# Folding layer norm and the q/k/v projection into one-hot tables, with the slots of a step filled anew and the stack loads moved to mid-step

## What is computed

```python
nesting, segments = _syntax_info(ids)              # two small integers per token: 16 and 8 values
h = concat(pos_table[s], nest_table[nesting], seg_table[segments]) @ W
qkv = layernorm(h) @ qkv_w.T + qkv_b               # 8 heads of 16 channels
attn = softmax(q @ k.T / 4)                        # 512 x 512 per head
h = h + (attn @ v) @ out_w.T + out_b
h = h + mixture_of_4_experts(layernorm(h))         # relu, low rank, gates
```

## Time and profile before

| | before |
|---|---|
| median of 3 runs | 1200.86 us |
| the profiled execution's own time | 1200.39 us |
| its span (first to last instruction) | 1198.6 us |
| PE busy | 1112.8 us, 93% of the span |
| DVE busy | 910.2 us, 76% |
| ACT busy | 823.0 us, 69% |
| POOL busy | 592.8 us, 49% |
| granted TensorE clock, mean | 0.973 |

### The profile page before, as it was taken

One profiled execution on the slowest core, in us unless ns is written; L12 is line 12 of the kernel. 1 busy time (PEld: TensorE's weight loads), 2 busy tenths in 40 slices (PEclk: granted clock), 3 DMA queues, 4 the chain that ended last, 5 costly groups with the idle time before them and its releaser, 6 DMA issues.

```text
span 1198.6 us, 20409 instructions
## 1 busy us (share of the span) xinstructions
PE 1112.8 (93%) x6392; PEld 455.6 (38%) x6392; DVE 910.2 (76%) x2370; ACT 823.0 (69%) x1602; POOL 592.8 (49%) x588
## 2 busy tenths in 40 slices
PE   2579999999999999999999999999999999999975
PEld 1223334444344434434344444443443444433322
DVE  6288888877888788777888887778888877788322
ACT  0217777777777777777777777777777777777841
POOL 2644555456544555565445655654455555622231
PEclk9669999999999999999999999999999999999997
DMA  3534534545454345454444455444444454441111
GB/s 84 130 81 97 123 88 113 120 110 123 103 120 105 102 106 119 116 120 105 117 107 102 102 120 125 111 107 114 112 102 100 118 127 109 109 102 44 54 56 36
DMA packets 88377, 123.98 MB, mean 103 GB/s; under 512 B 17469, under 2 KB 69054, under 8 KB 82054
## 3 DMA queue, kind: packets, MB, share of 16 engines
q1 hardware_dynamic: 86720, 121.08, 43.0%
q10 hardware_dynamic: 1550, 1.59, 0.5%
HBM read 80.81 MB, written 34.95 MB: 97 GB/s over the span
## 4 chain that ended last, share of the span: by engine, by line
PE 59%; DVE 20%; issue 4%; DMA 1%; POOL 1%; ACT 0%; SPq 0%; POOLq 0%; DVEq 0%
PE pv L635 14%; PE mix L645 12%; PE sc L624 11%; DVE negmax L882 11%; PE mix L697 7%; PE mix L662 4%; PE mix L713 3%; PE mix L702 2%; PE mix L680 2%; PE mix L657 2%; DVE out_sb L961 2%; DVE rden L901 1%; PE mix L673 1%; DVE onehot L861 1%; DVE mres L892 1%
## 5 line engine op out<-in xcount | busy, mean ns | idle before, releaser
L882 DVE TENSOR_REDUCE negmax<-mix 128x1 f32<-128x512 f32 x1024 | 669.9, 680 | 173.3 <-PE mix L645 166.2
L507 ACT ACTIVATE probs<-sc 128x512 f32<-128x512 f32 x1024 | 576.8, 598 | 183.8 <-PE sc L624 179.4
L624 PE MATMUL sc<-qstk,kstk 120*128 120x512 bf16 x1024 | 366.8, 381 | 0.8 <-ACT probs L507 0.6
L645 PE MATMUL mix<-kstk,qstk 96*128 96x512 bf16 x1024 | 357.2, 392 | 10.0 <-DVE negmax L882 4.8
L635 PE MATMUL pv<-probs,vals 128*32 128x512 f32 x2048 | 274.0, 601 | 0.0
L645 PEld LDWEIGHTS mix<-kstk,qstk 96*128 96x128 bf16 x1024 | 99.7, 98 | 347.2 <-DVE negmax L882 198.1
L460 POOL TENSOR_TENSOR ctxh<-ctx_sb,rdenb 128x512 f32<-128x512 f32 x64 | 81.3, 1271 | 258.7 <-DMA rdenb<-rden_dram 258.2
L624 PEld LDWEIGHTS sc<-qstk,kstk 120*128 120x128 bf16 x1024 | 99.5, 98 | 106.1 <-issue 36.6
L697 PE MATMUL mix<-xn2T,fc1T_sb 128*128 128x512 f32 x256 | 131.9, 599 | 0.0
L416 POOL TENSOR_TENSOR hb_sb<-h_sb,obias 128x512 f32<-128x512 f32 x32 | 40.7, 1273 | 121.6 <-DVE h L907 121.6
L565 ACT ACTIVATE hid<-mix 128x512 f32<-128x512 f32 x128 | 76.8, 600 | 24.2 <-PE mix L697 24.2
(11 more groups left out here) (116 smaller groups left out, 1067.8 us busy)
## 6 DMA issues: line engine op xcount, KB each, us to landing
stack_dram<-pieces SPq DMA_DIRECT2D x192, 128.0 KB
rdenb<-rden_dram SPq DMA_DIRECT2D x64, 256.0 KB
qstk<-stack_dram SPq DMA_DIRECT2D x32, 384.0 KB, 6.6
kstk<-stack_dram SPq DMA_DIRECT2D x32, 384.0 KB, 8.7
qstk<-stack_dram SPq DMA_DIRECT2D x32, 256.0 KB, 6.9
kstk<-stack_dram SPq DMA_DIRECT2D x32, 256.0 KB, 9.3
wrow<-w_dram SPq DMA_DIRECT2D x32, 256.0 KB
out<-out_sb SPq DMA_DIRECT2D x32, 256.0 KB, 2.7
```

Of the source, the lines that this page charges most:

```text
L507: act.activation(probs[:, c % 8, i % 2], sc[:, i % RING], ACT.Exp).then_inc(s_exp, 1)
L624: pe.matmul(sc[:, i % RING, :], kstk[0:KROWS, u, h, j * P:(j + 1) * P], qstk[0:KROWS, u, h, :], start=True, stop=True).then_inc(s_score, 1)
L645: pe.matmul(max_bank(m), qstk[0:STK, u, h, j * P:(j + 1) * P], kstk[0:STK, u, h, :], start=True, stop=True).then_inc(s_mxmm, 1)
L882: dve.tensor_reduce(negmax[:, m // NT, m % NT:m % NT + 1], max_bank(m), AX.X, ALU.max, negate=True).then_inc(s_max, 1)
```

## The change

Layer norm is linear but for rstd, so (row - mean) @ W is taken ahead: at the start the position table and the one-hot table are multiplied by the centred weights (`qkvC`), and per sequence q, k and v come from the one-hot matrix by one bfloat16 matmul each over 96 rows, with no transpose. DVE adds the position part of q and k, POOL multiplies by rstd, ACT adds the bias. For that, rstd, which lies along partitions, has to lie along the free axis: PE turns it (one more matmul in the "mT" product), ACT copies it (`rT`), SP stores it (`rstd_out`) and loads it back on all partitions (`rstd_in`). v keeps its tokens on partitions and is handled by POOL alone (`value`). `stack_dram` has two buffers. The products, and the work of ACT and DVE, stand in other slots; the stack loads stand behind `rden_in`, and wait in addition for the first "max" matmul of the sequence before. The steps begin one earlier (-5), with lists of their own for the first steps (`SP_FILL`, `POOL_FILL`). Cut to its core:

```diff
 PRODUCTS = [
-    ("project", -2), ("xnT", 3), ("q", 3), ("low", -3), ("k", 3), ("xn2T", -2), ("out", -3), ("gates", -2),
-    ("turn_gates", -2), ("v", 3), ("fc1_0", -2), ("embed", 4), ("mT", 1), ("fc1_1", -2), ("fc1_2", -2), ("fc1_3", -2),
+    ("project", -2), ("embed", 4), ("fc1_3", -3), ("low", -3), ("none", None), ("xn2T", -2), ("out", -3), ("gates", -2),
+    ("turn_gates", -2), ("fc1_0", -2), ("fc1_1", -2), ("mT", 1), ("q", 4), ("fc1_2", -2), ("k", 4), ("v", 4),
 ]
-BESIDE = {3: 3, 7: 7, 11: 12}
+BESIDE = (3, 7, 11)
 ACT_WORK = [
...
+    (1, 2, "qk", 3, 0), (2, 2, "relu", -3, 3), (3, 1, "qk", 3, 1), (4, 0, "ctx", -1, 1), (5, 2, "xn2T", -2, 0),
+    (8, 0, "gates", -2, 0), (9, 0, "gate_exp", -2, 0), (9, 1, "relu", -2, 0), (10, 1, "relu", -2, 1),
+    (12, 0, "rT", 4, 0), (12, 0, "mT", 1, 0), (12, 0, "ctx", 0, 0), (12, 1, "wT", -2, 0), (13, 1, "relu", -2, 2),
+    (15, 2, "v", 4, 0),
 ]
 DVE_WORK = [
...
+    (2, 1, "add_pos", 4, 0), (3, 0, "stats1", 4, 0), (3, 1, "stats1", 4, 1), (4, 0, "weigh", -3, 0),
+    (5, 0, "moments1", 4, 0), (6, 1, "finish", -3, 0), (7, 1, "invert_den", -1, 0),
+    (8, 1, "gate", -2, 0), (9, 1, "gate", -2, 1), (10, 0, "gate", -2, 2), (10, 0, "gate", -2, 3),
+    (13, 0, "add_qk", 4, 0), (15, 0, "add_qk", 4, 1), (15, 2, "hot", 5, 0),
 ]
 POOL_WORK = [
...
+    ("scale", 3, 0), ("add_bias", 3, 0), ("scale", 3, 1), ("rstd2", -2, 0), ("norm2", -2, 0),
+    ("second", 3, 0), ("residual", 3, 0), ("third", 3, 0), ("rstd1", 4, 0),
+    ("second", 3, 1), ("residual", 3, 1), ("third", 3, 1), ("normalise", -1, 0), ("v", 3, 0),
 ]
 SP_WORK = [
...
+    ("piece", 3, (0, 0)), ("piece", 3, (1, 0)), ("den_out", -1, 1), ("piece", 3, (0, 1)), ("den_in", -1, 0),
+    ("piece", 3, (0, 2)), ("ids", 5, 0), ("out", -3, 0), ("piece", 3, (1, 1)), ("rden_out", -1, 0), ("piece", 3, (1, 2)),
+    ("rden_in", -1, 0), ("stack", 3, 0), ("stack", 3, 1), ("rstd_out", 4, 0), ("den_out", 0, 0), ("max_in", 1, 0), ("weights_out", -2, 0),
+    ("rstd_in", 4, 0), ("weights_in", -2, 0),
+]
...
             def load_qstack(b, u):
                 upto(sp, s_pcout[0], b, 48)
                 upto(sp, s_score, b - U, TILES)
+                upto(sp, s_mxmm, b - 1, 32, 1)
...
+            def store_rstd(b):
+                upto(sp, s_rT, b)
+                upto(sp, s_rstdin, b - 1, 16)
+                sp.dma_start(rstd_dram, rT).then_inc(s_rstdout, 16)
+
+            def load_rstd(b):
+                upto(sp, s_scaled, b - 1, 2)
+                upto(sp, s_rstdout, b, 16)
+                sp.dma_start(rstdb[:], rstd_dram.rearrange("j p -> (j p)").partition_broadcast(P)).then_inc(s_rstdin, 16)
...
-            def norm(b):
+            def scale(b, side):
+                upto(pool, s_rstdin, b, 16)
+                upto(pool, s_raw, b, 2, side + 1)
+                pool.tensor_tensor(qk32[:, side, :], qk32[:, side, :], rstdb[:], ALU.mult).then_inc(s_scaled, 1)
+
+            def value(b, u):
+                upto(pool, s_v32, b)
...
+                pool.tensor_tensor(v32[:], v32[:], posV[:].rearrange("p j (h c) -> p j h c", h=NH),
+                                   ALU.add).then_inc(s_vpos, 1)
...
+                for g, col in ((0, 0), (1, HC)):
+                    pool.tensor_tensor(vals[:, u, :, 4 * g:4 * g + 4, col:col + HC], v32[:, :, 4 * g:4 * g + 4],
+                                       rstd1[:, b % 2].unsqueeze(2).unsqueeze(3).broadcast_to([P, NT, 4, HC]),
+                                       ALU.mult).then_inc(s_v, 1)
...
             def copy_qk(b, side):
-                upto(act, (s_qmm, s_kmm)[side], b)
...
-                act.activation(qk32[:, side, :], aux("qk"[side], 1), ACT.Identity,
-                               bias=(qb_sb[:], qkb_sb[:, 1:2])[side], scale=(QSCALE, 1.0)[side]).then_inc(s_qk32, 1)
+                upto(act, s_scaled, b, 2, side + 1)
+                act.activation(qk32[:, side, :], qk32[:, side, :], ACT.Identity,
+                               bias=(qb_sb[:], qkb_sb[:, 1:2])[side]).then_inc(s_qk32, 1)
...
+            def copy_rT(b):
+                upto(act, s_rTmm, b)
+                upto(act, s_rstdout, b - 1, 16)
+                act.copy(rT, aux("mT", 1)[2 * Q:2 * Q + NT, 0:P]).then_inc(s_rT, 1)
...
             def qk(b, side):
-                upto(pe, s_xnT, b)
-                pe.matmul(aux("qk"[side], 1), qkvT_sb[:, side, :], xnT[:], start=True, stop=True).then_inc((s_qmm, s_kmm)[side], 1)
+                upto(pe, s_hot, b)
...
+                pe.matmul(aux("qk"[side], 1), table[:, 1 + side], onehot[:], start=True, stop=True).then_inc((s_qmm, s_kmm)[side], 1)
...
             def v(b):
-                upto(pe, s_xnT, b)
+                upto(pe, s_hot, b)
                 for j in range(NT):
-                    mm = pe.matmul(aux("v")[:, j, :], xnT[:, j * P:(j + 1) * P], qkvT_sb[:, 2, :], start=True, stop=True)
+                    mm = pe.matmul(aux("v")[:, j, :], onehot[:, j * P:(j + 1) * P], table[:, 3], start=True, stop=True)
...
+            def turn_rstd(b):
+                upto(pe, s_rstd1, b)
+                pe.matmul(aux("mT", 1)[2 * Q:2 * Q + NT, 0:P], rstd1[:, b % 2], id32[:],
+                          start=True, stop=True).then_inc(s_rTmm, 1)
...
+            def add_qk(b, side):
+                upto(dve, (s_qmm, s_kmm)[side], b)
...
+                dve.tensor_tensor(qk32[:, side, :], aux("qk"[side], 1), posQK[:, side, :], ALU.add).then_inc(s_raw, 1)
```

More of the change, by code:

```diff
@@ L79 @@
+    ("second", 3, 0), ("residual", 3, 0), ("third", 3, 0), ("rstd1", 4, 0),
+    ("second", 3, 1), ("residual", 3, 1), ("third", 3, 1), ("normalise", -1, 0), ("v", 3, 0),
 ]
 SP_WORK = [
-    ("ids", 4, 0), ("piece", 3, (0, 0)), ("den_out", -1, 1), ("piece", 3, (0, 1)), ("piece", 3, (0, 2)),
-    ("den_in", -1, 0), ("piece", 3, (1, 0)), ("piece", 3, (1, 1)), ("out", -3, 0), ("piece", 3, (1, 2)),
-    ("rden_out", -1, 0), ("rden_in", -1, 0), ("den_out", 0, 0), ("max_in", 1, 0), ("weights_out", -2, 0),
@@ L84 @@
-    ("weights_in", -2, 0), ("stack", 3, 0), ("stack", 3, 1),
+    ("piece", 3, (0, 0)), ("piece", 3, (1, 0)), ("den_out", -1, 1), ("piece", 3, (0, 1)), ("den_in", -1, 0),
[3 more added lines that the diff above has]
+]
+SP_FILL = [
+    ("ids", 5, 0), ("piece", 3, (0, 0)), ("piece", 3, (1, 0)), ("piece", 3, (0, 1)), ("piece", 3, (0, 2)),
+    ("piece", 3, (1, 1)), ("rstd_out", 4, 0), ("rstd_in", 4, 0), ("piece", 3, (1, 2)), ("stack", 3, 0), ("stack", 3, 1),
+    ("max_in", 1, 0),
+]
@@ L283, in steps @@
         def steps(eng, step):
-            for t in range(-4, NSEQ + 3):
+            for t in range(-5, NSEQ + 3):
                 step(t, t % U)
@@ L387, in _ @@
                 "out": lambda b, u, _: store_out(b),
+                "rstd_out": lambda b, u, _: store_rstd(b),
+                "rstd_in": lambda b, u, _: load_rstd(b),
             }
             def step(t, u):
-                for name, ahead, part in SP_WORK:
+                for name, ahead, part in (SP_FILL if t < -1 else SP_WORK):
                     if runs(t + ahead):
@@ L481, in step @@
             def step(t, u):
-                for name, ahead, part in POOL_WORK:
+                for name, ahead, part in (POOL_FILL if t < -1 else POOL_WORK):
                     if runs(t + ahead):
@@ L611, in _, with fold_positions @@
             pe.wait_ge(s_const, 3)
+            def fold_positions():
+                pe.wait_ge(s_setcp, 4)
+                for side in range(2):
+                    pe.matmul(sc[:, 1 + side], qkvC[:, side], posWT, start=True, stop=True).then_inc(s_fold2mm, 1)
+                for j in range(NT):
+                    mm = pe.matmul(pv[:, j * P:(j + 1) * P], posWT[:, j * P:(j + 1) * P], qkvC[:, 2], start=True, stop=True)
+                mm.then_inc(s_fold2mm, 1)
             def scores_T(b, i, u):
@@ L629, in values @@
                 g, half = r // 2, r % 2
+                if r == 0 and jj == 0:
+                    upto(pe, s_v, b, 2)
                 if jj == 0:
@@ L739, in mix_user @@
                     name, ahead = PRODUCTS[c]
+                    if name == "none":
+                        return -1, (s_h, 1, 1)
                     if name == "mT" and runs(t - 2):
                         return t - 2, (s_wT, 1, 1)
+                    if name == "mT" and not runs(t + 1):
+                        return t + 4, (s_rT, 1, 1)
                     return t + ahead, products[name][1]
@@ L780, in step @@
                             row_tile(t, u, c, i)
-                        if what == "product" and c not in BESIDE.values():
+                        if what == "product" and c not in BESIDE:
                             product(t, c)
```

236 lines of the change are left out of this document (148 added, 88 removed).

## The result

| | before | after |
|---|---|---|
| median of 4 runs each | 1200.44 us | 1265.22 us (1257.82 to 1271.28) |
| ratio | | 1.0536, 95% interval 1.0497 to 1.0575 |
| the profiled execution's own time, its span | 1200.39, 1198.6 us | 1271.28, 1269.5 us |
| a steady step | 34.13 us | 36.13 us, uneven |
| granted TensorE clock, mean | 0.973 | 0.946 |

What follows compares the result with a forecast made beforehand. PE was taken to set the 34.13 us step; its work and waits and two transfer loops all gave 32.3 to 32.4, so 32.5 was taken. 26 steps save 42 us: 1158 us forecast, range 1130 to 1212.

Steps and rivals of the forecast that it cites:

- PE's saving: Transposes gone and q, k, v as cheap bfloat16 products: 2.49 us a step less, 0.11 added for turning rstd.
- new stalls: PE's new waits for readers of its result buffers: 1.2 us a step in sum, between 0 and 2.
- the four that were named: PE's waits in slots 9 (0.25 us), 15 (about 0.5), 1 (0.2) and 3 (0.25, low-rank product behind a relu).
- PE alone: The step if only PE's work and waits set it: 32.3 us, or 31.1 without the new waits.
- the landing behind the stack: On SP's queue, a small store behind the stack lands 10.4 to 13.4 us after the stack's first issue; 11.9 taken.
- d: Time from the stack's first issue to rstd on all partitions: 14.5 us taken, slower than before from 16.2 on.
- loop 1: First score tile to stack's first issue, 19.9 us, then 12.5 until the maxima land: 32.4 us a step.
- loop 2: rstd's landing through POOL to the stack's first issue, 17.9 us, then 14.5 until rstd returns: 32.4 us a step.
- the ends: Time before and after the steady steps: taken as even, with -4 to +6 us.
- C: Rival: rstd returns too late behind the stack; 26 us per us of step, around 35 us a step, 1223 us; chance 0.20.
- B: Rival: the DMA order costs nothing and PE alone decides; 31.6 us a step, 1135 us; chance 0.24.
- DVE's rise to 29.4 us: DVE's work per step grows from 28.0 to 29.4 us by adding positions to q and k, staying under 31.1.

Runs made afterwards that it cites:

- e13: Changed kernel with stack loads last, three readers of PE's buffers called earlier, and POOL's rstd1 moved so POOL idles while DVE cuts the maxima: 1132.05 us.
- e12: Changed kernel, with k's stack loads bringing one head of eight from the fifth sequence on, same instructions and waits: 1202.46 us.
- e3: Changed kernel, with POOL scaling q and k by a constant tile so that no engine waits for rstd, all transfers kept: 1266.08 us.
- e4: Changed kernel, with rstd's store and load and the maxima's load issued by ACT on its own DMA queue: 1276.93 us.

## Why the prediction was wrong

**PE's saving: nearly right, and its new stalls taken too small.** q, k and v cost 0.21 to 0.23 us in the changed kernel (q from 656.21 to 656.42, k from 661.14 to 661.36, v from 662.23 to 662.46 in PE's timeline), as read from the earlier trace rows; in sum PE works 2.0 us a step less, where 2.49 - 0.11 = 2.38 was taken, and 0.4 of it was not traced. The new stalls were put at 1.2 us, between 0 and 2; with the stack last they are 2.23. Three of the four that were named are there: 0.25 in slot 9 as taken, and 0.51 and 0.67 in slots 15 and 1 for 0.5 and 0.2; the one in slot 3 is not among the waits. One was not seen: the maximum of slot 13 behind the weights' copy, 0.80, which ACT makes after the maxima's and the context's. Nor was it seen that the stall in slot 9 grows to 1.2 when POOL runs there. "PE alone" was 32.3 in the prediction and is 33.78 in the run with the stack last, so by this term alone the change would have come out at 1198 us, the same as before, and not at the 1158 forecast; e13, with these waits out, has 31.78, near the 31.1 that the prediction gave without stalls.

**The step that failed: the landing behind the stack.** "Behind the stack a small store lands 10.4 to 13.4 us after the stack's first issue. I take the middle, 11.9." It landed at 14.6, past the upper end. The maxima, put at 12.5, landed at 15.4; d, put at 14.5, was 18.0. The other halves of the loops were right: 17.6 us from rstd to S for 17.9, and 20.2 from the maxima to S for 19.9. So loop 1 is 35.6 and not 32.4, loop 2 likewise. The range was the error, and the middle of it the more so. Its upper end, 13.4, was the landing of the stack's own last transfer, and a store behind it was not given a later one. In the changed kernel the stack itself landed later (KB, median us from issue to landing):

```profile
kstk<-stack_dram SPq DMA_DIRECT2D x32, 128.0 KB, 11.2
```

With its issue put at about 653.35, an estimate from the three issues that begin at 652.31, that is S + 14.2, just ahead of the store's 14.6. e12 shows that the bytes in front set it. The ids, whose landings the prediction read the earlier trace rows, bear it out: behind the stack the two loads took 8.5 and 9.6 us in the median, and 2.4 and 2.3 in the changed kernel, where they are issued 6 us ahead of it.

The steps account for 26 x (36.13 - 32.5) = 94 of the 113 us by which the profiled execution missed. The other 19 lie in the ends, taken as even with -4 to +6: 1271.28 - 26 x 36.13 = 332 against 1200.39 - 26 x 34.13 = 313. Of these, 12 are lost before the fourth cut of the maxima (at 174.50 us, and at 162.48 in the kernel before) and 3.5 after the last one (88.5 us to the end of the span for 85.0); why was not tested.

**The rivals.** C named the place, and its threshold was met: it decides from d = 16.2 on, and its step at the slow end, 35.3, is close to 36.13. Its signs are in the profile (POOL waits 8.34 us for rstd; SP's queue waits for rstd's store, which takes 9.3 us to land, a little under the 10 that C named). It had 0.20 of the chances. But C blamed rstd's round trip alone; e3 shows that the maxima behind the stack do the same by themselves, so its price of 26 us per us of d would not have come back if rstd had been made faster. The ring order that was cited for it is not the cause shown: e4 took the transfers out of that order, and they landed 0.2 us (rstd's store) and 0.7 us (the maxima) sooner. B's condition (what stands behind the stack costs nothing) is nearly what e12 sets up, and there PE's waits still kept the step at 33.80 and not 31.6.

**A rule that was missed.** DVE's rise to 29.4 us was counted, but not that DVE stands still behind POOL. In the fill of the kernel before it was to be seen: the same cast took 0.96 us beside an operation of POOL:

```profile
76.97 0.96 DVE L890 CAST mpc<-negmax 128x32 bf16<-128x32 f32 x1
```
```profile
76.74 1.15 POOL L444 TENSOR_TENSOR pieces<-qkr,pieces 128x512 bf16<-128x512 f32 x1
```

In the changed kernel it is this, too, that makes slot 9 wait 1.23 us (DVE and POOL):

```profile
647.07 1.19 DVE L1021 TENSOR_TENSOR mres<-negmax,mpc 128x32 f32<-128x32 f32 x1
```
```profile
647.06 1.16 POOL L490 TENSOR_TENSOR pieces<-qkr,pieces 128x512 bf16<-128x512 f32 x1
```

The rows show more than that it happens: the reciprocal (one small input) keeps its 0.34 us and the maxima read from PE's buffers their 0.68 while POOL runs; casts from 32-bit to 16-bit, the comparison `hot`, and operations with two inputs in SBUF are the ones held, if POOL's operation began first. The Trainium skill's page "SBUF — State Buffer", section "Who interferes with whom", states that a DVE operation with two SBUF inputs contends with a GpSimd operation that reads SBUF, that casts and tensor-scalar operations can do so as well, in the modes that use both ports, that whoever issues first keeps the shared ports for the whole instruction, and that one with a single SBUF input outside those modes does not contend. The trace agrees on the two-input operations, the reciprocal and the maxima; that the casts and `hot` ran in such a mode would fit, and no row shows the mode. In the changed kernel the wait is covered by the longer loops over the transfers; with the stack last it decides whether 32.7 or 31.8 us a step are reached.
